# Cross-attention keys stacked in four groups of four heads instead of two of eight

## The reference

```
q = w8a8_linear(x, wq, bq)            # 32 x 100 x 256, 16 heads of 16
k = cond @ wk.T + bk                  # 32 x 1444 x 256
v = cond @ wv.T + bv
scores = q k^T / sqrt(16) + mask      # per head 100 x 1444
o = softmax(scores) @ v
out = w8a8_linear(o, wo, bo)
```

## Time and profile before

| | us |
|---|---|
| median of 3 runs | 3969.43 |
| the profiled execution | 3973.11 |
| its span, first to last instruction | 3971.4 |
| TensorE matmuls busy | 3606.3 (91%) |
| VectorE busy | 2420.2 (61%) |
| ScalarE busy | 1700.7 (43%) |
| mean granted TensorE clock | 0.925 |

### The profile page before, as it was taken

The page is one execution under the profiler, slowest core; times in us unless marked ns, Lnnn a source line. Parts: engine busy times, 40 slices in busy tenths (PEclk is TensorE's granted clock), DMA queues, the critical chain, the costliest instruction groups (busy, mean ns, idle before and its releaser), DMA issues. The chain is left out here.

```text
span 3971.4 us, 94397 instructions
## 1 busy us (share of the span) xinstructions
PE 3606.3 (91%) x34556; PEld 2673.7 (67%) x34556; DVE 2420.2 (61%) x5690; ACT 1700.7 (43%) x2883; POOL 629.0 (16%) x664
## 2 busy tenths in 40 slices
PE   7999999995899999998999999999999968888887
PEld 6989899895566666665666666566666636666666
DVE  4444444445576776766767676676766746665565
ACT  3222232222455554554545555454555534333332
POOL 0000000002111111111101111011111102333222
PEclk9999999997999998999989999898998978988999
DMA  3000000001554646464564646546464521000000
GB/s 98 14 13 12 4 8 12 12 9 41 96 110 85 125 84 120 77 121 88 89 115 81 121 84 106 105 84 119 76 122 87 97 48 41 13 12 12 21 12 13
DMA packets 122425, 257.11 MB, mean 65 GB/s; under 512 B 19140, under 2 KB 99852, under 8 KB 118972
## 3 DMA queue, kind: packets, MB, share of 16 engines
q1 hardware_dynamic: 113744, 244.11, 32.7%
q10 hardware_dynamic: 8300, 7.69, 0.7%
HBM read 99.95 MB, written 9.83 MB: 28 GB/s over the span
## 5 line engine op out<-in xcount | busy, mean ns | idle before, releaser
L1385 DVE CUSTOM_DVE_ANT_0 ca_rowmax<-ca_rowmax,ca_msk 100x420 f32<-100x420 f32 (+1 forms) x1024 | 923.9, 926 | 577.3 <-PE ca_rowmax L1168 572.0
L1109 ACT ACTIVATE ca_prob<-ca_unit 128x800 f32<-128x800 f32 x768 | 640.3, 834 | 466.3 <-PE ca_unit L1292 464.8
L1168 PE MATMUL ca_rowmax<-ca_ks,ca_qs 96*100 96x512 bf16 (+1 forms) x1536 | 535.2, 427 | 92.5 <-DMA ca_ks<-ca_ks 68.0
L1292 PEld LDWEIGHTS ca_unit<-ca_qs,ca_ks 99*128 99x128 bf16 (+1 forms) x6144 | 385.0, 104 | 250.7 <-issue 169.9
L1292 PE MATMUL ca_unit<-ca_qs,ca_ks 99*128 99x100 bf16 (+1 forms) x6144 | 463.2, 220 | 31.1 <-issue 16.4
L1255 PE MATMUL ca_acc<-ca_prob,ca_vaug 128*17 128x100 f32 x12288 | 469.4, 269 | 16.5 <-issue 9.1
L1002 POOL TENSOR_TENSOR ca_key_part<-ca_key_rest,ca_key_part 128x512 bf16<-128x512 f32 (+1 forms) x192 | 209.9, 1100 | 1594.8 <-ACT ca_key_part L1064 1594.8
L1150 PE MATMUL ca_ring<-ca_wvT,ca_ctxT 128*128 128x256 f32 (+1 forms) x1536 | 381.6, 390 | 3.2 <-DVE ca_key_rest L1359 1.6
L1141 PE MATMUL ca_ring<-ca_ctxT,ca_wkT 128*128 128x512 f32 (+1 forms) x768 | 345.9, 573 | 2.4 <-DVE ca_key_rest L1359 2.4
L1168 PEld LDWEIGHTS ca_rowmax<-ca_ks,ca_qs 96*100 96x100 bf16 x1536 | 166.2, 133 | 250.6 <-issue 177.6
L1255 PEld LDWEIGHTS ca_acc<-ca_prob,ca_vaug 128*17 128x17 f32 x12288 | 247.4, 101 | 118.4 <-issue 53.7
(11 more groups left out here) (275 smaller groups left out, 6252.1 us busy)
## 6 DMA issues: line engine op xcount, KB each, us to landing
ca_ks<-ca_key_part SPq DMA_DIRECT2D x768, 90.2 KB, 4.1
ca_ks<-ca_ks SPq DMA_DIRECT2D x64, 722.0 KB, 7.4
ca_ctx<-in_ctx SPq DMA_DIRECT2D x32, 1408.0 KB
ca_ks<-ca_ks SPq DMA_DIRECT2D x64, 361.0 KB, 9.4
ca_msk<-in_mask_BxSxS_ff SPq DMA_DIRECT2D x32, 564.1 KB
sa_w_stage<-in_L_attn_w_qkv SPq DMA_DIRECT2D x12, 512.0 KB, 5.2
sa_x_in<-in_x ACTq DMA_DIRECT2D x8, 400.0 KB
sa_x_res<-in_x SPq DMA_DIRECT2D x8, 400.0 KB
```

The source lines that it names most:

```text
L1109: act.activation(prob[:, 2 * (p % 2):2 * (p % 2) + 2, :], unit[:, :, 0:QUAD * N], ACT.Exp)\
L1168: last = pe.matmul(rowmax[0:N, s0:s1], qs[0:STACK, par, h, :], ks[0:STACK, par, h, s0:s1], start=True, stop=True)
L1292: return pe.matmul(unit[0:rows(t0 + k), k, j * N:(j + 1) * N], ks[:, par, h, keys(k)], qs[:, par, h, :], start=(j == 0), stop=True, skip_g ...
L1385: dve.tensor_tensor_reduce(rowmax[0:N, s0:s1], rowmax[0:N, s0:s1], msk[:, par, s0:s1], 1.0, -3.0e38, ALU.add, ALU.max, top[:, bank, h:h + ...
```

## The change

The keys are stacked in four groups of four heads. `put` copies all three parts of a group (6 DMAs as before in size), `repeat` copies within a group, so that its two DMAs are half as large (361 and 180 KB). There are 24 puts and 8 repeats in a turn, in place of 24 and 4. The order is: puts of groups 0 and 1, repeats of 0, puts of 2, repeats of 1, puts of 3, repeats of 2, the next context, repeats of 3. Groups 0 and 2 share the semaphores `placed[0]` and `stacked[0]`, groups 1 and 3 the others; for that reason the repeats of groups 2 and 3 first wait until those of groups 0 and 1 have landed. TensorE waits at heads 0, 4, 8 and 12 (rounds 15, 21, 2 and 9).

```diff
--- before.py
+++ after.py
@@ -698,7 +698,8 @@
         return all_pieces[:2] if kind == "mh" else all_pieces[2:]
 
 
-    HALF = H // 2
+    GROUP = QUAD
+    GROUPS = H // GROUP
     PER_QUAD = TILES // 2
     PAIRS = NQ * PER_QUAD
     assert TILES % 2 == 0
@@ -833,8 +834,9 @@
         mask_loaded = sem("mask_loaded")
         xq_loaded, xr_loaded = sem("xq_loaded"), sem("xr_loaded")
         hi_out, parts_out, mid_out = sem("hi_out"), sem("parts_out"), sem("mid_out")
-        placed = [sem(f"placed{k}") for k in range(H // HALF)]
-        stacked = [sem(f"stacked{k}") for k in range(H // HALF)]
+
+        placed = [sem(f"placed{k}") for k in range(2)]
+        stacked = [sem(f"stacked{k}") for k in range(2)]
         q_step = sem("q_step")
         ints_done, qry_done = sem("ints_done"), sem("qry_done")
         split_step = sem("split_step")
@@ -852,8 +854,12 @@
 
         O_STEPS = 9
         O_HALF = 7
-        PLACED = 16 * HALF // C * PARTS
+        PLACED = 16 * GROUP // C * PARTS
         STACKED = 16 * 2
+
+        def wait_stacked(eng, group, b):
+
+            eng.wait_ge(stacked[group % 2], STACKED * (GROUPS // 2 * b + group // 2 + 1))
 
         def one(tensor, b):
 
@@ -870,32 +876,39 @@
 
             def stack(b, par, more):
 
-                def put(half, parts):
-                    for part in parts:
-
+                def put(group):
+
+                    for part in range(PARTS):
                         standing_wait(sp, (hi_out, mid_out, parts_out)[part], 6 * (b + 1), sp_passed)
-                        for n in range(half * HALF // C, (half + 1) * HALF // C):
+                        for n in range(group * GROUP // C, (group + 1) * GROUP // C):
                             sp.dma_start(ks[DH * part:DH * (part + 1), par, n * C:(n + 1) * C, :],
-                                         key_part[DH * n:DH * (n + 1), part, :, :]).then_inc(placed[half], 16)
-
-                def repeat(half):
-                    heads = slice(half * HALF, (half + 1) * HALF)
-                    standing_wait(sp, placed[half], PLACED * (b + 1), sp_passed)
+                                         key_part[DH * n:DH * (n + 1), part, :, :]).then_inc(placed[group % 2], 16)
+
+                def repeat(group):
+
+                    heads = slice(group * GROUP, (group + 1) * GROUP)
+                    standing_wait(sp, placed[group % 2], PLACED * (GROUPS // 2 * b + group // 2 + 1), sp_passed)
+                    if group >= 2:
+                        wait_stacked(sp, group - 2, b)
+                        sp.sem_inc(sp_passed, 1)
                     sp.dma_start(ks[3 * DH:5 * DH, par, heads, :], ks[0:2 * DH, par, heads, :])\
-                        .then_inc(stacked[half], 16)
+                        .then_inc(stacked[group % 2], 16)
                     sp.dma_start(ks[5 * DH:6 * DH, par, heads, :], ks[0:DH, par, heads, :])\
-                        .then_inc(stacked[half], 16)
-
-                put(0, (0, 1, 2))
-                put(1, (0,))
+                        .then_inc(stacked[group % 2], 16)
+
+                put(0)
+                put(1)
                 repeat(0)
-                put(1, (1, 2))
+                put(2)
+                repeat(1)
+                put(3)
+                repeat(2)
                 if more:
 
                     bn.wait_full(sp, ("ct", 2, C - 1), b)
                     sp.sem_inc(sp_passed, 1)
                     load_ctx(b + 1)
-                repeat(1)
+                repeat(3)
 
             def store(b):
                 standing_wait(sp, out_ready, b + 1, sp_passed)
@@ -1052,8 +1065,8 @@
                     s, w = third(k), third(k).stop - third(k).start
                     bn.wait_full(act, task, b)
                     if (k, c) == (0, 0) and not (isinstance(b, int) and b == 0):
-                        for k in range(H // HALF):
-                            act.wait_ge(placed[k], PLACED * b)
+                        for k in range(2):
+                            act.wait_ge(placed[k], PLACED * GROUPS // 2 * b)
                     act.activation(key_part[:, 0, c, s], ring[bn.bank(task)][:, 0:w], ACT.Identity,
                                    bias=bk_col[:, c:c + 1]).then_inc(hi_out, 1)
                 elif task[0] == "km":
@@ -1161,8 +1174,8 @@
                     h = task[1]
                     if kind == "mh" and h == 0:
                         bn.wait_all_out(pe, [("qs", 0), ("qs", 1)], b)
-                    if kind == "mh" and h % HALF == 0:
-                        pe.wait_ge(stacked[h // HALF], STACKED * (b + 1))
+                    if kind == "mh" and h % GROUP == 0:
+                        wait_stacked(pe, h // GROUP, b)
                     bm.wait_empty(pe, task, b)
                     for s0, s1 in pieces(kind):
                         last = pe.matmul(rowmax[0:N, s0:s1], qs[0:STACK, par, h, :], ks[0:STACK, par, h, s0:s1],
```

## The result

The changed kernel takes 3796.27 us (median of 4 runs, 3790.34 to 3802.54) against 3970.4 us for the kernel before on the same chip (3964.13 to 3976.74). The profiled execution takes 3797.85 us, its span is 3796.1.

The account below looks back on a forecast made before the run. It took TensorE's stop of about 2.2 us a turn at head 0, and the half clock after it, as the bound. Stops -63, clock -85, turn 0 -4 and context +49 gave -103: 3867 us, range 3805 to 3955.

Parts of the forecast that it names:

- Steps (1) to (3): Queue before head 0: fewer puts ahead, half-size repeats, a small issue hole; group 0 lands at T0+16.3, not T0+22.4.
- Step (4): TensorE's added waits at heads 4, 8 and 12: all met by earlier landings, so they cost nothing.
- (5): Context transposes: the context lands at T0+38.7, wanted at T0+38.6; mean cost 1.6 us a turn, +49 us in 30.
- The clock: TensorE in the 30 turns: of 334 us at half speed all but 50 goes, -85 us.
- The stops: TensorE's waits at head 0 for the copies: all 29 in the 30 turns go, -63 us.
- Turn 0: The turn before the 30: its remaining stop of 5.2 us, counted as -4 us.
- clean gain: Rival at the context transposes: the context is always early enough, -152 us, 3817 us; chance 0.15.
- the context takes over: Rival at the context transposes: context lands at T0+40, every turn waits 1.4 us, half lose their clock, 3943 us; chance 0.17.
- the slower one: Rival at the context transposes: context lands at T0+41.4, costing 6.7 us a turn, 4018 us; chance 0.08.
- The clock falls all the same: Rival on TensorE's clock: the stop at head 0 goes but the clock still falls, 3914 us; chance 0.08.

Follow-up runs that it names:

- e3: The changed kernel with all 24 puts ahead of the first repeats, groups still small, each with its own semaphores; 4020.41 us.
- e4: The changed kernel with the load of the next context behind the repeats of the last group; 3803.22 us.
- e5: The kernel before with four filler products of no use on TensorE just ahead of head 0; 3921.54 us.
- e8: The changed kernel with eight groups of two heads in place of four groups of four; 3825.07 us.
- e7: The changed kernel with 30 turns in one pass of the loop in place of 10; 3768.96 us.
- e1: The kernel before with 12 puts instead of 16 ahead of the first repeats, halves and full-size repeats kept; 3901.24 us.
- e6: The kernel before with 12 puts ahead of the first repeats and each repeat cut into two DMAs of four heads; 3883.6 us.
- e2: The kernel before with eight filler products of no use on TensorE just ahead of head 0; 3977.68 us.

## Why the prediction fell short, step by step

Steps (1) to (3), group 0's landing, were right in kind: forecast T0+16.3 (15.6 to 17.1; with the longest hole of 0.7 us and the upper rate the sum gives 17.4), measured 15.3 in the mean. e3 shows the cause by undoing it. Step (4) was right: no wait at heads 4, 8 or 12 in 30 turns, with group 1 at T0+22.9 (24.9 forecast) and group 2 at 29.6 (33.5).

**The step that failed is (5), "what is late next: the context", +49 us in the sum; it measured 0.7.** The moment at which TensorE wants it was right (38.6 forecast, 38.5 measured). The landing was not: 38.7 forecast, 36.5 measured. Up to the third pair I was 3.9 us late. The 12th put came 0.6 us sooner than I counted; a half pair took 3.6, 3.7 and 3.1 us (15.3 - 11.7, and behind puts 18 and 24, which land at 19.2 and 26.5), 3.45 in the mean and not 4.0, which is 1.65 us over three; and 12 puts behind a pair came (19.2 - 15.3)/6 = 0.65 and (26.5 - 22.9)/6 = 0.6 us apart and not 0.77, 1.8 us. I had read the 0.8 us between the first puts as the rate of the transfer. It is not: SyncE issues those puts 8.43/12 = 0.70 us apart, and puts behind a pair of copies, with the queue full, land faster than that. What spaces the first ones by 0.8 was not tested. Where the queue is full, puts and pairs move at nearly the same rate, 90.2/0.62 = 145 KB/us, and 541/3.45 = 157 KB/us, against 146 for the full pair. The 5.2 us for a half pair that the prediction works out from the Trainium skill (DMA: Bandwidth & Descriptors, section Anatomy of one DMA) rest on a figure for DMAs that GpSimd issues, and are further from the 3.45. The context itself took 6.9 us behind the pair and not 5.2, which gave 1.7 us of it back. And the price was too high: I let one turn in five wait 3 us and lose its clock; e4, with the context at T0+38.6 on average, has 11 waits of 1.9 us at most, and pays 12 us with their clock.

**The clock**, -85 in the sum, was right in kind (e3, e5) and too small: -109.6, because a microsecond at half clock costs 0.39 us and not 0.3, which I had read from only two turns with small differences, and 280 us of it went and not 284.

**The stops**, -63, measured -62.8. Turn 0, -4, measured -1.7. Two terms were missing inside the 30 turns: TensorE, now ahead, waits 17.5 us more for VectorE (35.1 against 17.6), and 2.3 more for ScalarE; "issue" fell by 5.5, from 26.7 (the 21.4 of my prediction left out a third line, 5.3 us before L1168). Outside them 16.1 us went: 10.5 before the cross-attention and 5.6 after its 31st turn. The first I take for no effect of the change, since the code there is the same: in the ten profiled executions that stretch takes 996.6 to 1007.1 us, and the two kernels happen to lie at its ends, with 44.4 and 64.9 us at half clock. No step of the forecast is about it: that part of the gain is luck. Of the 5.6, 5.0 lie in the last turn, where TensorE's idle pieces fall by 5.9 us: 3.4 us of "issue" waits are gone, and 3.1 of waits for ScalarE. Why they went was not tested. The sum: -62.8 - 109.6 - 1.7 + 0.7 - 5.5 + 17.5 + 2.3 - 16.1 = -175.2.

So the kernel went the way of the rival *clean gain* (-152, 0.15), with a dearer clock. The rivals in which the context takes over, and the slower one, needed it at T0+40 or later; it reached that neither here (39.5 at most) nor in the mean of e8 (39.0). *The clock falls all the same* is refuted: 38 us at half clock are left in 30 turns, all but 3.4 of them (turn 29) in turns with an "issue" wait, and none in e7.

What stays open: whether the waits for VectorE could be taken away too, why a microsecond at half clock costs 0.37 to 0.39 us here and not another share, and what part of the "issue" waits hangs on the length of the rows.

## What to carry to other kernels

When a queue of DMAs feeds an engine in order, cut the group that is waited for first, so that its last copy is issued while the queue is still full: the order alone brought 1.8%, the order with small groups 4.4%. Count what stands behind by the rate of a full queue, not by the spacing of the first, unhurried DMAs. A short stop of TensorE in every turn is worth its own length and what the half clock after it takes; here the second was 1.7 times the first, and useless work in the gap already won 1.3%.

## What the runs showed of the hardware

- With copies in rows of 23 KB under way at the wrong moment, packets of instructions begin 2.7 to 4.2 us later than with the same bytes in rows of 11.5 KB, and TensorE has 53.8 us of "issue" waits in place of 15.5 (e1, e6).
- A small DMA among others of a full queue costs about its bytes and 0.1 us (e8), though alone a put takes 3.1 us to land.
- The first turn of a new pass of the loop has 6.2 + 1.7 and 4.1 + 1.8 us of "issue" waits and takes 8.7 and 10.4 us longer than a plain one; without it the clock is 1.00 in all 30 turns (e7).
- A product of 128x256 in f32 stands in the trace as two passes, 16 records for 8 products and 3.72 us (e2).
